# Sums over the partitions: GpSimd's all-reduce in place of a product with ones on TensorE

## The reference, cut to what matters

```python
scores = jnp.clip(scores, -80.0, 80.0)
scores = jnp.where(causal[None, None], scores, -jnp.inf)
weights = jax.nn.softmax(scores / jnp.sqrt(jnp.float32(d_qk)), axis=-1)
attn = jnp.einsum('bhqk,bhkd->bhqd', weights, v)
```

## Time and profile before

| what | value |
|---|---|
| median of 3 runs | 1409.7 us (1409.53 to 1411.36) |
| profiled execution | 1410.6 us |
| its span, first to last instruction | 1409.1 us |
| PE busy | 1372.4 us, 97% |
| DVE busy | 1147.5 us, 81% |
| ACT busy | 782.2 us, 56% |
| POOL busy | 124.2 us, 9% |
| mean granted clock of TensorE | 0.993 |

### The profile page before, as it was taken

The page is one execution under the profiler, slowest core; times in us unless marked ns, Lnnn a source line. Parts: engine busy times, 40 slices in busy tenths (PEclk is TensorE's granted clock), DMA queues, the critical chain, the costliest instruction groups (busy, mean ns, idle before and its releaser), DMA issues.

```text
span 1409.1 us, 27675 instructions
## 1 busy us (share of the span) xinstructions
PE 1372.4 (97%) x9810; PEld 1155.4 (82%) x9810; DVE 1147.5 (81%) x1339; ACT 782.2 (56%) x861; POOL 124.2 (9%) x175
## 2 busy tenths in 40 slices
PE   7999689999999999999999999999999999999998
PEld 6888568788888888888978889888899688878887
DVE  7666378898898898989889898898789878967664
ACT  4232356766666666675666666666666756532221
POOL 0000111201101101000010100111100011012121
PEclk9999899999999999999999999999999999999999
DMA  7332665544434332424242332444422233165652
GB/s 292 119 100 79 190 196 160 165 148 137 136 93 141 96 121 84 131 72 144 63 123 86 90 118 65 119 145 148 132 60 64 75 109 116 38 197 179 185 159 90
DMA packets 110769, 174.91 MB, mean 124 GB/s; under 512 B 9608, under 2 KB 65160, under 8 KB 108168
## 3 DMA queue, kind: packets, MB, share of 16 engines
q1 hardware_dynamic: 93880, 108.99, 25.0%
q0 software_dynamic: 16016, 63.80, 15.6%
q10 hardware_dynamic: 832, 1.57, 0.5%
HBM read 125.83 MB, written 48.50 MB: 124 GB/s over the span
## 4 chain that ended last, share of the span: by engine, by line
PE 75%; DVE 8%; ACT 3%; DMA 1%; issue 1%; POOL 0%; ACTq 0%; DVEq 0%
PE score_ps L1248 29%; PE out_ps L1270 19%; PE score_ps L1367 4%; PE score_ps L1369 4%; PE score_ps L1368 4%; DVE prob_l L1564 2%; ACT prob_h L1427 2%; DVE prob L1551 1%; PE out_ps L1289 1%; DVE prod L1523 1%; PE out_ps L1290 1%; PE out_ps L1293 1%; PE score_ps L1218 1%; ACT prob L1421 1%; PE score_ps L1219 1%
## 5 line engine op out<-in xcount | busy, mean ns | idle before, releaser
L1427 ACT CAST prob_h<-prob 128x1024 fp32r<-128x1024 f32 (+1 forms) x288 | 289.6, 1005 | 236.9 <-DVE prob L1546 189.2
L1564 DVE TENSOR_TENSOR prob_l<-prob,prob_h 128x1024 fp32r<-128x1024 f32 (+1 forms) x288 | 336.0, 1167 | 39.6 <-ACT prob_h L1427 38.2
L1248 PE MATMUL score_ps<-q_h,key_slot 64*128 64x512 f32 x1792 | 363.3, 389 | 0.0
L1421 ACT ACTIVATE prob<-score_ps 128x1024 f32<-128x1024 f32 (+1 forms) x288 | 281.9, 979 | 140.6 <-PE score_ps L1248 92.3
L1270 PE MATMUL out_ps<-prob_h,value_slot 64*128 64x512 f32 (+1 forms) x1792 | 350.4, 377 | 1.8 <-DMA value_slot<-values 0.4
L1559 DVE TENSOR_TENSOR total<-total,prob 128x1024 f32<-128x1024 f32 (+1 forms) x256 | 294.9, 1152 | 0.0
L1270 PEld LDWEIGHTS out_ps<-prob_h,value_slot 64*128 64x128 f32 x1792 | 179.8, 184 | 35.7 <-DVE prob_l L1564 7.5
L1546 DVE TENSOR_SCALAR prob<-prob 128x1024 f32<-128x1024 f32 x224 | 155.1, 693 | 65.8 <-ACT prob L1421 65.5
L1248 PEld LDWEIGHTS score_ps<-q_h,key_slot 64*128 64x128 f32 x1792 | 180.0, 185 | 26.8 <-issue 5.0
L1248 PE MATMUL score_ps<-q_l,key_slot 64*128 64x512 f32 x896 | 181.1, 388 | 0.0
L1248 PE MATMUL score_ps<-rot_hh,key_slot 64*128 64x512 f32 x896 | 180.9, 387 | 0.0
(11 more groups left out here) (210 smaller groups left out, 2007.4 us busy)
## 6 DMA issues: line engine op xcount, KB each, us to landing
key_slot<-keys SPq DMA_DIRECT2D x144, 256.0 KB, 2.7
value_slot<-values SPq DMA_DIRECT2D x144, 128.0 KB, 2.4
rot_hh<-turned POOLq DMA_DIRECT2D x30, 512.0 KB, 6.2
heads_rows<-head_rows POOLq DMA_DIRECT2D x15, 1024.0 KB, 9.7
turned<-rot_hl POOLq DMA_DIRECT2D x14, 1024.0 KB, 5.2
rows<-heads_rows SPq DMA_DIRECT2D x28, 512.0 KB, 5.5
rot_l<-turned POOLq DMA_DIRECT2D x30, 256.0 KB, 7.7
x_in<-in_x SPq DMA_DIRECT2D x16, 256.0 KB, 2.6
```

The costliest lines, as they stand in the source:

```text
L1248: mm = pe.matmul(score_ps[:, half, c * 512:(c + 1) * 512], keys_of[ROWS[r], :], moving[par][ROWS[r], half * HW + c * 512:half * HW + (c + ...
L1421: nc.scalar.activation(prob[half][:, 0:width], score_ps[:, half, 0:width], ACT.Exp, scale=QK_SCALE).then_inc(exp_done, 1)
L1427: nc.scalar.copy(prob_h[half][:, 0:width], prob[half][:, 0:width]).then_inc(high_done, 1)
L1564: nc.vector.tensor_tensor(p_l, p, p_h, ALU.subtract).then_inc(split, 1)
```

## The change

`sum_up` and `read_sums` remain for the last unit alone. For units 0 to 14 GpSimd adds the buffer `total` up over the partitions, in place, every partition then holding the sum, and the first row goes to memory. The wait for DVE's last addition moves from PE to POOL, and ACT begins a unit's buffer only after the sums of the unit two before are in memory.

```diff
+            added = pool.alloc_register("added")
+            pool.reg_mov(added, 4)
-            def store(n):
+            def store(n, par, couple):
+                if isinstance(couple, int):
+                    pool.wait_ge(summed, 4 * couple * couple + (1 - par) * (4 * couple + 2))
+                else:
+                    pool.wait_ge(summed, added)
+                    pool.reg_add(added, added, 4 * couple + 2)
                 pool.wait_ge(out_read, 2 * n + 2)
                 pool.dma_start(one_of(heads_out, n), head_rows[:, :]).then_inc(heads_stored, 16)
-                pool.wait_ge(sums_read, n + 1)
-                pool.dma_start(one_of(sums_out, n).rearrange("(q g) t -> q (g t)", g=2),
-                               sums[0:P:32, :]).then_inc(sums_stored, 16)
+                nc.gpsimd.partition_all_reduce(total[par][:, :], total[par][:, :], P, REDUCE_ADD).then_inc(reduced, 1)
+                pool.wait_ge(reduced, n + 1)
+                pool.dma_start(one_of(sums_out, n).rearrange("h t -> (h t)").unsqueeze(0), total[par][0:1, :]).then_inc(sums_stored, 16)
...
-            pool.wait_ge(summed_up, UNITS - 1)
+            pool.wait_ge(sums_stored, 16 * (UNITS - 1))
...
                 if kind == CORNER:
-                    if prev is not None:
-                        pe.wait_ge(summed, unit.added)
-                        pe.wait_ge(out_read, 2 * n - 1)
-                        sum_up(1 - par, out_ps[:, 0, :])
...
                     pe.wait_ge(values_in, 16 * (t + 1))
-                    since(pe, sums_read, n)
+                    since(pe, out_read, 2 * n - 1)
                     weigh(t, 0, slot, CORNER, False)
...
                 def begin(half):
-                    since(act, summed_up, n - 1)
+                    since(act, sums_stored, 16 * (n - 1))
                     act.wait_ge(clipped, 2 * t + half + 1)
...
                 if prev is not None:
-                    read_sums(n - 1, out_ps[:, 0, :])
                     act.wait_ge(weighed, 2 * t)
                     read_out(n - 1, 1)
```

More of the change, by code:

```diff
@@ L20 @@
 F32R = mybir.dt.float32r
+REDUCE_ADD = bass.bass_isa.ReduceOp.add
 P = 128
@@ L906, in attend_and_combine @@
         summed_up = sem("summed_up")
+        reduced = sem("reduced")
         sums_read = sem("sums_read")
@@ L1094, in _, with during @@
                     nc.gpsimd.memset(chunks(raw(rot_l0[n][rest, :]))[:, :, c, :], 0.0).then_inc(zeroed, 1)
-            def store(n):
+            added = pool.alloc_register("added")
[6 more added lines that the diff above has]
+                    pool.reg_add(added, added, 4 * couple + 2)
                 pool.wait_ge(out_read, 2 * n + 2)
                 pool.dma_start(one_of(heads_out, n), head_rows[:, :]).then_inc(heads_stored, 16)
-                pool.wait_ge(sums_read, n + 1)
-                pool.dma_start(one_of(sums_out, n).rearrange("(q g) t -> q (g t)", g=2),
-                               sums[0:P:32, :]).then_inc(sums_stored, 16)
+                nc.gpsimd.partition_all_reduce(total[par][:, :], total[par][:, :], P, REDUCE_ADD).then_inc(reduced, 1)
+                pool.wait_ge(reduced, n + 1)
+                pool.dma_start(one_of(sums_out, n).rearrange("h t -> (h t)").unsqueeze(0), total[par][0:1, :]).then_inc(sums_stored, 16)
             queries = pool.alloc_register("queries")
             pool.reg_mov(queries, 3)
-            def during(n, par, first=False, has_next=True, has_second=True):
+            def during(n, par, couple, first=False, has_next=True, has_second=True):
                 if has_next:
@@ L1116, in during @@
                 if not first:
-                    store(n - 1)
+                    store(n - 1, 1 - par, couple)
                 if has_second:
@@ L1121, in during @@
                                    raw(rot_hl[:, :, :, :]).rearrange("p w e n -> p w (e n)")).then_inc(passed, 16)
-            during(0, 0, first=True)
-            during(1, 1)
+            during(0, 0, 0, first=True)
+            during(1, 1, 0)
             with pool.Fori(1, COUPLES - 1) as m:
                 for par in range(2):
-                    during(2 * m + par, par)
+                    during(2 * m + par, par, m)
             pool.wait_ge(passed, 16 * (UNITS - 2))
@@ L1136, in _ @@
                 pool.dma_start(home, source).then_inc(weights_in, 16)
-            during(UNITS - 2, 0, has_second=False)
+            during(UNITS - 2, 0, COUPLES - 1, has_second=False)
             pool.wait_ge(sums_stored, 16 * EARLY)
             pool.dma_start(early_sums[:, :], sums_out[0:EARLY].rearrange("u h t -> (u h) t")).then_inc(early_in, 16)
-            during(UNITS - 1, 1, has_next=False, has_second=False)
+            during(UNITS - 1, 1, COUPLES - 1, has_next=False, has_second=False)
             pool.wait_ge(inverted, 1)
@@ L1399, in read_out, with read_sums @@
                                out_ps[:, 2 * half:2 * half + 2, :]).then_inc(out_read, 1)
-            def read_sums(n, bank):
-                act.wait_ge(summed_up, n + 1)
-                since(act, sums_stored, 16 * n)
+            def read_sums(bank):
+                act.wait_ge(summed_up, 1)
                 nc.scalar.copy(sums[:, :], bank[:, 0:512]).then_inc(sums_read, 1)
@@ L1496, in _ @@
                 read_out(UNITS - 1, half)
-            read_sums(UNITS - 1, score_ps[:, 0, DIM:2 * DIM])
+            read_sums(score_ps[:, 0, DIM:2 * DIM])
             gates(0, 0)
```

2 lines of the change are left out of this document (1 added, 1 removed).

## The result

The changed kernel takes 1504.8 us, median of 4 runs (1503.7 to 1505.5), against 1409.6 us for the kernel before in the same rounds: a ratio of 1.0671 [1.0653, 1.069]. It lies inside the range, at the upper end of rival 3 (held, but short).

The account below looks back on a forecast made before the run. PE was taken to bound the kernel. Held DVE clips cost 16.1 us in each of 13 units, 17.35 in unit 14 and 1.95 in unit 15, 228.6 on 1410.6: forecast 1638 us, range 1430 to 1780.

Parts of the forecast that it names:

- rival 3: DVE held, but reduction only 4.6 to 9.2 us, or DVE slips some operations in: 1416 to 1507 us, chance 0.13.
- the 14 long clips: Sign in the profile after: 14 of DVE's 32 clips some 15 us longer, ending 0.4 us after a reduction.
- 0.5 in the granted clock: Sign in the profile after: the lower clock level of 1.2 GHz behind each of some 14 holes in PE.
- ACT's new wait: ACT's first copy of unit 2 waits for unit 0's sums; expected covered, as everything behind moves some 16 us.
- Rivals 1, 2 and 4: Reduction fits beside DVE's work, 1394, 0.06; DVE not held, 1401 to 1408, 0.06; reduction above 27.6 us, over 1776, 0.09.
- T: Time of one POOL reduction over 2048 columns, estimated as eight passes of 2.30 us: 18.4 us.
- the bounds of 9.2 and 27.6: Ends for the reduction's time in us: half and one and a half times the estimate, giving 1507 and 1776 us.
- the clip ends at T + 0.4: In each corner DVE's held LATE clip ends 0.4 us after POOL's reduction ends, counted from POOL's start.
- The cover: DVE work between POOL's mark and the clip's usual end that hides the reduction: 3.5 us in units 1 to 13.
- The gain: Four products of 512 columns a unit leave PE: 1.1 us in each of 15 units, 16.2 us in all.
- The clock: PE's products run slower after each long stop, costing 1.9 us a stop.
- The loading of the code: 7.19 us before POOL's first broadcast moves before unit 1's reduction; taken as delayed, not added, at no cost.

Follow-up runs that it names:

- the late queue without a reduction: Changed kernel without the reduction; POOL's store instead waits for DVE additions lasting about as long: 1403.1 us, ratio 0.9945.
- the second reduction: Changed kernel plus an unneeded reduction of the 512 columns of `sums` behind the first in units 1 to 14: 1509.0 us, ratio 1.0707.
- half of the columns: Changed kernel with the reduction working on 1024 of 2048 columns, the other sums left out: 1425.3 us, ratio 1.0102.
- three quarters: Changed kernel with the reduction working on 1536 of 2048 columns, the other sums left out: 1477.5 us, ratio 1.0467.

## Why the prediction was right and wrong

**Right by its own steps.** DVE's operations with two SBUF inputs are held, those from PSUM are not; PE stands for nearly all of it; 13 of the 14 long clips are there, and in unit 1 `rot_hl` is held in place of the 14th; 0.5 in the granted clock behind each stop. In unit 15 the reduction is covered (at 1209.33, with a clip of 0.69 us at 1224.56). The turned queries are late for no one, and ACT's new wait bit once, for 0.8 us. POOL's queue costs nothing (the late queue without a reduction). Rivals 1, 2 and 4 fall: T is 11.82 us, and DVE is held.

**The term that failed first: T.** "Seven halvings, each a pass over the 2048 columns at the broadcast's rate, and one more" made 18.4 us; it measured 11.82, so 6.6 us a unit too much. No row of before could settle it; the bounds of 9.2 and 27.6 held it, but they too were shares of a guess.

**The step that failed beside it: "the clip ends at T + 0.4".** I took the rule from two broadcasts, where DVE ended 0.40 us after POOL. A reduction lets a two-input operation go after 9.2 us, not 11.8: 2.6 us a unit. With the measured T in the prediction's own sum, each unit is 6.6 us less, 13 x 9.5 + 10.8 for unit 14, and unit 15 gains the 1.1: 133 us, or 1543. With the hold of 9.2 it loses 14 x 2.6 = 36 more, which gives 1507, against the measured 1505. The Trainium skill (SBUF — State Buffer, Who interferes with whom) speaks of a lock for the whole instruction, and does so of DVE's two-port modes; I took it for the two-input operations too, of which it says only that they contend with a GpSimd instruction that reads SBUF. By a lock for the whole instruction the clip would have ended at 629.6 and not at 627.40. The measurement decides: it is held for the first four fifths.

**Smaller terms.** The cover was 4.1 us in place of 3.5 (the clip, unheld, would have ended at 621.88, 4.09 after POOL's start at 617.79), and 3.8 in every other unit. The gain was 0.5 us in the mean and 0.8 to 0.9 in the typical unit, in place of 1.1: the four products did stand on PE, but ACT and DVE set the end of the corner. From ACT's first copy to its rounding of the new queries it is 3.73 us before (555.07 to 558.80) and 3.26 after (612.23 to 615.49), and only ACT's copy of the sums, 0.48, has gone. The clock cost about 1.2 to 1.6 us a stop, not 1.9; the two go against each other, and some 0.3 us is left of them. Together the typical unit went from the 16.1 of the prediction to 6.1: 6.6 for T, 2.6 for the hold, 0.3 to 0.6 for the cover and that 0.3.

**What was costed at nothing and wasn't.** The loading of the code, "delayed, not added to", costs some 3 us, about as much as the runs can tell: the late reduction of unit 1 meets another two-input operation of DVE, `rot_hl`. In units 2 to 4 the cover is shorter by 0.9 to 2.4 us (lateness 7.61, 6.45 and 7.90 against 5.5), since POOL comes late to the reduction, its gather having waited for the turned queries.

The range held, through rival 3, to which I gave 0.13. Its condition was T up to 9.2; it came true through the length of the hold, 9.2 of 11.82. That this hold equals the bound 9.2, and the measured time the 1507 computed from it, is luck: the bound was half of an estimate of T that was too long.

No version beats the kernel before. The most that can be won is 8 us, and a reduction within the cover of 4.1 us has room for fewer than 900 of a unit's 2048 columns (896 were already 0.35 to 0.68 us late).

## What to carry to other kernels

An idle engine is only free if what it runs takes nothing from the others: ask for each long GpSimd instruction which of DVE's operations meets it first, and whether that one has two inputs in SBUF. Put such work where DVE reads PSUM, and cut it to that length. What is held behind it is paid by the engine that waits for DVE: here nearly every microsecond of the clip's lateness was one of PE, with the clock on top, while the hold by the second reduction, beside slack, cost nothing. And what a removed instruction is worth is read from the chain that sets the end of its stage (here ACT's), not from its length on the busiest engine.

## What the runs showed of the hardware

GpSimd's all-reduce (float32, addition) costs 0.4 us plus 5.6 ns a column, the same for 32 and for 128 partitions (11.87 us at 2048 columns; 3.23 at 512). It holds a two-input operation of DVE for the first four fifths: the clip came free 4.5, 5.0, 7.3 and 9.6 us after POOL's start at 896, 1024, 1536 and 2048 columns, where the reductions took 5.3, 6.1, 8.9 and 11.8. Fast one-input operations it holds in two stretches, 9.2 us and 2.7 us, with only the end of one and the start of the next between them.

What a stop of PE costs in clock does not go by the stop's length. In the typical corners it cost nothing behind 0.6 to 0.9 us (half of the columns), 2.4 us behind 2.9 and 1.2 behind 3.2 (three quarters), and 1.2 to 1.6 behind 5.2 to 5.5 (the changed kernel), where the lower level began during the stop and half of it was over when PE went on.
